# A transformer block with a conditioned conv on one core: order of the first loads, and where the modulation and the first weight parts are made

## What is computed

```python
x = x + conv(x, cond[:, None, :])                  # 32 taps, 256 channels, each by itself, padded left by 31
ada = (cond @ ada_w + ada_b)[:, None, :]           # 6 parts of 256
shift1, scale1, gate1, shift2, scale2, gate2 = jnp.split(ada, 6, axis=-1)
x1 = ln(x) * (1.0 + scale1) + shift1
q, k, v = split(x1 @ qkv_w + qkv_b)                # 256 -> 3 * 2048
a = softmax(q @ k.T * scale) @ v                   # in each sequence of 32 tokens
z = x + gate1 * (a @ out_w + out_b)
x2 = ln(z) * (1.0 + scale2) + shift2
z = z + gate2 * (gelu(x2 @ ffn_w1 + ffn_b1) @ ffn_w2 + ffn_b2)
return x + z
```

## Time and profile before

| | us |
|---|---|
| median of 3 runs | 334.86 (332.93 to 335.1) |
| the profiled execution, whole | 335.84 |
| its span, first to last instruction | 334.0 |
| TensorE busy | 304.7 |
| DVE / ACT / GpSimd busy | 147.5 / 155.2 / 77.1 |
| mean granted clock of TensorE | 0.959 of 2.4 GHz |

### The profile page before, as it was taken

How to read it: one execution, slowest core, us unless ns; L and a number is a source line. 1 busy time by engine, 2 the same in 40 slices (tenths; PEclk the granted TensorE clock), 3 DMA queues, 4 the chain that set the end, 5 groups by cost and what they waited for, 6 DMA issues and landing times.

```text
span 334.0 us, 7536 instructions
## 1 busy us (share of the span) xinstructions
PE 304.7 (91%) x3279; PEld 257.7 (77%) x3279; DVE 147.5 (44%) x235; ACT 155.2 (46%) x259; POOL 77.1 (23%) x68
## 2 busy tenths in 40 slices
PE   0644989999999979999999999999999999899994
PEld 0644879888888868888888888888888687588884
DVE  0612383375344306225332532531625699783232
ACT  3333314555267243536625525644453547742910
POOL 4200185310063020015303005401102345420400
PEclk9955789999999997999999999999999999999999
DMA  6780042010023001003201101210200000000011
GB/s 203 196 312 4 4 126 65 4 65 0 2 72 118 0 4 63 2 0 108 82 0 27 36 0 63 84 45 0 65 2 1 2 2 0 0 2 0 0 65 63
DMA packets 10056, 15.74 MB, mean 47 GB/s; under 512 B 837, under 2 KB 6061, under 8 KB 9901
## 3 DMA queue, kind: packets, MB, share of 16 engines
q1 hardware_dynamic: 9712, 15.24, 14.4%
q10 hardware_dynamic: 317, 0.10, 0.1%
HBM read 14.26 MB, written 1.11 MB: 46 GB/s over the span
## 4 chain that ended last, share of the span: by engine, by line
PE 82%; DVE 9%; DMA 4%; issue 4%; ACT 0%; SPq 0%; POOL 0%; ACTq 0%
PE bank L975 17%; PE bank L976 17%; PE bank L977 17%; PE bank L1051 8%; PE bank L984 5%; PE bank L986 4%; PE bank L985 4%; PE bank L1037 3%; DMA cond_padded<-zrows 2%; PE bank L881 2%; PE bank L911 2%; DMA pool<-cond_padded 2%; PE bank L897 1%; DVE yacc L774 1%; DVE pt L677 1%
## 5 line engine op out<-in xcount | busy, mean ns | idle before, releaser
L302 POOL TENSOR_TENSOR wl<-raw,wh 128x512 fp32r<-128x512 f32 x40 | 52.3, 1330 | 167.5 <-ACT wh L361 167.5
L975 PE MATMUL bank<-x1h,wl 128*128 128x512 f32 (+1 forms) x176 | 67.5, 383 | 1.5 <-DVE x1l L630 1.5
L976 PE MATMUL bank<-x1l,wh 128*128 128x512 f32 (+1 forms) x176 | 65.8, 374 | 0.0
L977 PE MATMUL bank<-x1h,wh 128*128 128x512 f32 (+1 forms) x176 | 65.8, 374 | 0.0
L434 ACT ACTIVATE pool<-bank,bg 128x512 f32<-128x512 f32 x56 | 38.6, 689 | 58.4 <-PE bank L977 58.1
L688 DVE SCALAR_TENSOR_TENSOR ol<-bank,bT,oh 128x512 fp32r<-128x512 f32 x32 | 24.0, 750 | 51.2 <-ACT oh L463 50.2
L975 PEld LDWEIGHTS bank<-x1h,wl 128*128 128x128 f32 x176 | 33.8, 192 | 7.6 <-DVE x1l L630 1.6
L976 PEld LDWEIGHTS bank<-x1l,wh 128*128 128x128 f32 x176 | 34.0, 193 | 5.6 <-issue 0.2
L977 PEld LDWEIGHTS bank<-x1h,wh 128*128 128x128 f32 x176 | 33.9, 192 | 5.7
L1051 PEld LDWEIGHTS bank<-pt,pool 128*128 128x128 f32 x256 | 31.9, 191 | 3.4 <-DVE pt L677 0.8
L1051 PE MATMUL bank<-pt,pool 128*128 128x128 f32 x256 | 32.8, 276 | 0.6 <-DVE ol L688 0.4
(11 more groups left out here) (108 smaller groups left out, 419.2 us busy)
## 6 DMA issues: line engine op xcount, KB each, us to landing
raw<-in_L_cond_qkv_w_dram SPq DMA_DIRECT2D x12, 512.0 KB, 3.9
raw<-in_L_cond_out_w_dram SPq DMA_DIRECT2D x4, 512.0 KB, 3.5
raw<-in_L_cond_ffn_w_dram SPq DMA_DIRECT2D x4, 512.0 KB, 3.5
pool<-in_x_dram SPq DMA_DIRECT2D x2, 512.0 KB, 4.2
pool<-cond_padded SPq DMA_DIRECT2D x4, 256.0 KB, 4.5
adaw<-in_L_cond_ada_w_dram SPq DMA_DIRECT2D x1, 1024.0 KB, 7.6
out_dram<-pool SPq DMA_DIRECT2D x4, 256.0 KB, 2.2
adaw<-in_L_cond_ada_w_dram SPq DMA_DIRECT2D x1, 512.0 KB, 6.3
```

The source lines that it names most:

```text
L302: g.tensor_tensor(wl[:, cols], raw[:, cols], wh[:, cols].bitcast(F32), ALU.subtract)\
L975: pe.matmul(dst, wl[:, w_cols], a_hi, start=start, stop=False)
L976: pe.matmul(dst, wh[:, w_cols], a_lo, start=False, stop=False)
L977: return pe.matmul(dst, wh[:, w_cols], a_hi, start=False, stop=stop)
```

## The change

- SP issues the two writes of `cond_padded` first, then x, then the Toeplitz input, and only then the first third of `adaw` and the biases. ACT's queue keeps the load of `crow`.
- SP waits for two blocks of the conv (`conv_blocks` at 2) before `load_group(0)`; the rest of `adaw` comes after it.
- The modulation has four parts: scale1, shift1, the middle third, the last third. The first two are made by TensorE after the conv, the last two inside `project_chunk(0, ...)`.
- The biases are transposed after conv block 1, into `S_BANK`; `turn(3)` stands behind the projections of q and half of k of chunk 0, `mean(0)` ahead of `turn(1)`.
- GpSimd makes the low parts of q and k ahead of `rstd(0)`. Those of v are made by DVE, and counted on a semaphore of their own (`s_vlow`); GpSimd adds them to `s_wlo`.

TensorE in the front, before: the biases and the modulation stand ahead of the conv (L881), mean(0) (L911) behind 64 of L897's (two turns; here and below each row of a plain f32 matmul is two passes).

The diff, cut to its core:

```diff
-        ADA_PARTS = [(0, ADA1), (ADA1, 2 * ADA1), (2 * ADA1, ADA)]
-        ADA_BANKS = [YB[1], OB[1], YB[1]]
-        ADA_STEPS = [1, 3, 4]
+        ADA_PARTS = [(CT, 2 * CT), (0, CT), (ADA1, 2 * ADA1), (2 * ADA1, ADA)]
+        ADA_BANKS = [OB[0], OB[1], YB[1], OB[1]]
+        ADA_STEPS = [1, 3, 4, 5]
...
+            sp.dma_start(pad_rows(0, T), cond.rearrange("k (g s) -> k g s", g=QB)).then_inc(s_pad, 16)
+            sp.wait_ge(s_zr, 1)
+            sp.dma_start(pad_rows(T, 2 * T - 1), zrows[:, :].rearrange("k (g s) -> k g s", g=QB)).then_inc(s_pad, 16)
             for n in range(HALVES):
                 sp.dma_start(xtok[:, 4 * n:4 * n + 4, :], x_v[:, 4 * n:4 * n + 4, :]).then_inc(s_x[n], 16)
-            load_adaw(0, 0, ADA1 * P)
-            for at, src in ((B_QKV, qkv_b), (B_ADA, ada_b), (B_OUT, out_b), (B_F1, ffn_b1), (B_F2, ffn_b2)):
...
             sp.wait_ge(s_pad, 32)
             for g in range(QB):
                 sp.dma_start(toep_in[T * g:T * (g + 1), :, :].rearrange("p u s -> p (u s)"),
...
+            load_adaw(0, 0, ADA1 * P)
+            for at, src in ((B_QKV, qkv_b), (B_ADA, ada_b), (B_OUT, out_b), (B_F1, ffn_b1), (B_F2, ffn_b2)):
...
+            sp.wait_ge(s_cv, 2)
+            load_group(0)
             load_adaw(1, ADA1 * P, ADA * P)
-            load_group(0)
...
# GpSimd
+            g.wait_ge(s_xq[2], len(SPREADS_POOL))
+            low_parts(0, range(0, 4))
             rstd(0)
-            low_parts(0, range(0, 4))
+            g.wait_ge(s_vlow, 2)
+            g.wait_ge(s_wlo, 4)
+            g.sem_inc(s_wlo, 2)
             rstd(1)
-            low_parts(0, range(4, 6))
...
# ACT
-            a.wait_ge(s_bt, 1)
-            a.activation(bT[:, :], CB[2][:, 0:NBIAS], ACT.Copy).then_inc(s_btc, 1)
...
             conv_copy(0)
+            a.wait_ge(s_bt, 1)
+            a.activation(bT[:, :], S_BANK[:, 0:NBIAS], ACT.Copy).then_inc(s_btc, 1)
+            high_parts(0, range(0, 2))
             conv_copy(2)
-            high_parts(0, range(0, 4))
+            high_parts(0, range(2, 6))
+            group_biases(0, 0, 3)
             xc_copy(0)
-            group_biases(0, 0, 3)
             squares(0)
-            xc_copy(2)
-            high_parts(0, range(4, 6))
             squares(1)
             x1_high(0)
+            xc_copy(2)
...
# DVE
+            for p in (4, 5):
+                cols = slice(PIECE * p, PIECE * (p + 1))
+                v.wait_ge(s_whi, p + 1)
+                v.tensor_tensor(wl[:, cols], raw[:, cols], wh[:, cols].bitcast(F32), ALU.subtract).then_inc(s_vlow, 1)
+            centre(0)
             xc_copy(1)
-            centre(0)
+            modulation(1)
             scale_up(0)
...
             x1_low(1)
+            xc_copy(3)
             modulation(2)
-            one_plus(2, SCALE2)
+            modulation(3)
+            one_plus(3, SCALE2)
             centre(2)
...
# TensorE
+            conv(0)
+            conv(1)
+            pe.wait_ge(s_row[1], 16 * 5)
+            pe.wait_ge(s_co[0], 1)
+            pe.transpose(S_BANK[:, 0:NBIAS], rows[:, :], ident[0:NBIAS, 0:NBIAS]).then_inc(s_bt, 1)
+            conv(2)
+            conv(3)
+            pe.wait_ge(s_adaw[0], 16)
+            pe.wait_ge(s_co[1], 1)
+            modulation(0)
             turn(0)
+            mean(0)
             turn(1)
-            mean(0)
-            turn(2)
+            modulation(1)
             var(0)
             mean(1)
             spread(0)
-            pe.wait_ge(s_adaw[1], 16)
-            modulation(1)
-            turn(3)
+            turn(2)
             var(1)
...
             project_chunk(0, (0, 1))
             spread(1)
+            pe.wait_ge(s_xc[0], 2)
             project_chunk(0, (2,))
-            pe.wait_ge(s_co[1], 2)
+            turn(3)
+            pe.wait_ge(s_adaw[1], 16)
             modulation(2)
             project_chunk(0, (3,))
             pe.wait_ge(s_adat, ADA_STEPS[1])
+            modulation(3)
+            pe.wait_ge(s_adat, ADA_STEPS[3])
             mean(2)
```

More of the change, by code:

```diff
@@ L252, in _ @@
                     .then_inc(s_toep, 16)
+            load_adaw(0, 0, ADA1 * P)
+            for at, src in ((B_QKV, qkv_b), (B_ADA, ada_b), (B_OUT, out_b), (B_F1, ffn_b1), (B_F2, ffn_b2)):
+                n = src.shape[0] // P
+                sp.dma_start(rows[at:at + n, :], src.rearrange("(n p) -> n p", p=P)).then_inc(s_row[1], 16)
+            sp.wait_ge(s_cv, 2)
+            load_group(0)
             load_adaw(1, ADA1 * P, ADA * P)
-            load_group(0)
             with sp.Fori(1, NG) as hg:
@@ L723, in _ @@
                 v.tensor_copy(toep[:, blk, :].rearrange("p s u -> p u s"), toep_in[:, :, blk]).then_inc(s_tp[k], 1)
+            conv_copy(1)
+            conv_copy(3)
             v.wait_ge(s_btc, 1)
@@ L866, in _ @@
                               start=(i == 0), stop=False, is_transpose=True, skip_group_check=True)
-            pe.wait_ge(s_row[1], 16 * 5)
-            pe.transpose(CB[2][:, 0:NBIAS], rows[:, :], ident[0:NBIAS, 0:NBIAS]).then_inc(s_bt, 1)
             def conv(k):
-                if k == 2:
-                    pe.wait_ge(s_btc, 1)
                 if k == 3:
-                    pe.wait_ge(s_adat, 1)
+                    pe.wait_ge(s_cond, 1)
                 pe.wait_ge(s_tp[k], 1)
@@ L957, in _ @@
             pe.wait_ge(s_xq[2], len(SPREADS_POOL))
-            for k in range(NX):
-                conv(k)
+            conv(0)
[8 more added lines that the diff above has]
+            modulation(0)
             turn(0)
+            mean(0)
             turn(1)
-            mean(0)
-            turn(2)
+            modulation(1)
             var(0)
```

13 lines of the change are left out of this document (1 added, 12 removed).

## The result

| | before | after |
|---|---|---|
| median (of runs) | 334.98 us (4) | 337.26 us (4) |
| lowest to highest | 332.93 to 336.39 | 336.28 to 340.0 |
| ratio after/before, 95% | | 1.0112 [1.0058, 1.0166] |
| profiled execution, its span | 335.84, 334.0 us | 336.28, 334.5 us |

The forecast was 330.0 us, 1.5% less, in a range of 327.0 to 334.0; the change costs up to 1% instead. The two profiled executions differ by only 0.44 us.

What follows compares the result with a forecast made beforehand. TensorE's matmuls bound the kernel from 48 us, a chain of waits the 47 us ahead. Terms -3.4 - 0.2 - 3.0 - 1.6 + 3.3 = -4.9 us on 335.84 gave 330.9, as a median 330.0, range 327.0 to 334.0.

Steps and rivals of the forecast that it cites:

- step 1: Start of the conv: earlier pads and Toeplitz load bring the first conv matmul from 17.00 to 13.6, -3.4 us.
- step 2: Length of the conv: 14.7 us against 14.9, -0.2 us; the loaded code fetch moves from first to third round.
- step 3: Conv's end to first projection: 12.5 us instead of 15.5, -3.0 us, from low parts, mean(0), turn(1) and modulation.
- steps 4 and 5: First projection to mean(2): no clock fall, -1.6 us; turn(3) and a modulation moved behind the first projection, +3.3 us.
- rival C: Start of the conv: GpSimd's and the vector engine's copies of x obstruct each other, +3.7 us, 333.7; chance 0.07.
- rival E: Conv's third code fetch waits for the whole held weight load: 332.8 us; chance 0.07.
- (a): First norm: GpSimd's low parts run earlier, so the vector engine's shift and low part are no longer slowed, -3.0 us.
- (b): After the conv: mean(0) waits only for ACT's copy of the first turned part, not turn(1), -1.1 us.
- (c): Between mean(0) and var(0): turn(1) and modulation(1) take 2.1 to 2.7 us where 1.3 went by, +1.1 us.
- Rival F: TensorE stays at the lower clock from first projection through mean(2): +6.9 us, 336.9, slower than before; chance 0.04.
- step 5: Behind the first projection: turn(3), one modulation of 16 passes and a wait at mean(2) now cost time, +3.3 us.

Runs made afterwards that it cites:

- e2: Changed kernel with the pad-row writes put behind crow on ACT's queue and x first on SP's: 1.0001 of the kernel before.
- e1: Changed kernel with GpSimd's copies of x given to ACT (six in all) and the vector engine (ten): 1.0059 of the kernel before.
- e11: Kernel before with the two pad-row writes first on SP's queue and only crow's load on ACT's: 0.9997 of the kernel before.
- e9: Kernel before with e5's edit, e2's queues, Toeplitz ahead of modulation loads, first modulation between conv blocks 2 and 3: 0.9982 of the kernel before.
- e6: Changed kernel with pad rows behind crow on ACT's queue, weights not held, and turn(1) ahead of mean(0): 0.9973 of the kernel before.
- e8: Changed kernel run again with no edit: 1.0045 of the kernel before, median 335.87 us.
- e12: Changed kernel with modulation(2) and turn(3) put back ahead of the first projection: median 339.83 us beside 332.63 of the kernel before; no ratio given.
- e7: Changed kernel with only turn(1) put ahead of mean(0) again: 1.0065 of the kernel before.
- e3: Changed kernel without SP's wait for two conv blocks, so weights aren't held: 1.0034 of the kernel before.
- e4: Changed kernel with weights held until all four conv blocks are done, high and low parts moved later: 1.0048 of the kernel before.
- e5: Kernel before with only GpSimd's four low parts of q and k moved ahead of rstd(0): 0.9917 of the kernel before, median 331.76 us.
- e10: Changed kernel with modulation(0) and (1) between the third and fourth conv blocks: 1.0157 of the kernel before, four executions.

## Why the prediction was wrong

The forecast of 330.0 us missed the measured 337.26. In the profiled executions mean(2) came 6.7 us later than forecast (58.80 against 52.1): 4.4 us by step 1, 0.2 by step 2, 1.8 by step 3 and 0.2 by steps 4 and 5.

**Step 1 failed, by 4.4 us, the largest miss.** Its failing sentence is that the copies of x "no longer matter: the Toeplitz load is last". The pads were written by 5.15, inside the forecast's 4 to 6, and Toeplitz landed at 14.0 against 13.0. But x landed at 9.3, not 7.3. I put that to Toeplitz, issued at 5.15 and moving beside it: in e2, where it goes at 8.31, x is there at 6.6, though x itself is issued 1.2 us earlier there as well. And the copies took 7.96 instead of 4.96 us. That was rival C, which I gave 0.07 with a start of 17.3; measured 18.04. That its number comes so near is luck: it had x 1.9 us too early and the two sets of copies one after the other, 9.3 us, where they took 7.96. I argued against it from the pace of one copy alone, 0.62 us for 512 elements, when I had no row with both engines copying; e1 showed that this was no evidence. The Trainium skill (SBUF — State Buffer, Who interferes with whom) has the lock with GpSimd for copies only in a mode with two ports. Whether these copies are in that mode no run here shows; the rows of after, e2 and e11 (7.9 us each) against e1 (6.14 for ten) show a slowing of the vector engine's, whatever its mechanism, and GpSimd's took 1.3 us each in the first three, 1.04 in before.

No run brought step 1's 3.4 us. The earliest start was 15.56 (e9), 1.4 us before that of before. e1 and e9 start the conv 1.6 and 1.4 us earlier than after and before, and end it no earlier, or lose it to work placed there. e2 and e6 start it at 16.0 and 16.1 and end it at 31.3 and 31.4, before at 31.9. e2's ratio is 1.0001 against 1.0045 of e8, on another chip and with intervals that overlap: some half a per cent, if anything. So the collision explains why the conv started late; that it alone turned the sign isn't shown.

**Step 2 had the mechanism and under-sized a term.** The stops stand after 204, 127 and 127 pairs, the long one moved to the third round, as forecast. The third round took 6.1 us in e12, 6.36 in after and e2, 7.45 in e8 and e1 and 7.7 in e7, where one row had given 5.9: rival E's direction (0.07), a fetch that waits for the held load. e3 and e4 show that the load is the cause. In after's profile the two rounds ahead were 0.4 us quicker than forecast, so the length came out only 0.2 us over; in e8's the third round was another 1.1 us longer.

**Step 3 was right in (a), wrong in its price of modulation(0) and in (b), and (c) was at the upper end.** The shift and low part are at 0.75 and 0.76, 3.0 us as forecast. But modulation(0) didn't hide beside the conv's last copy, where I had it at 0.95 us and "costs nothing": it took 1.92 at the low pace, of which some 0.6 show (from the conv's end to turn(0) 1.77 us against 1.17). mean(0) took 2.08, priced by its 1.37 in before. (c), turn(1) and modulation(1), had 2.1 to 2.7 us, the low pace of the turn included; from the end of mean(0) to var(0) 2.6 went by. So modulation(0) and mean(0), priced by rows of a faster TensorE, make some 1.3 of the 1.8 us. The 16 passes of modulation(0) and (1) had stood at 13.47 in before, where TensorE waited for Toeplitz, and took 1.91 us there. Cut out of that hole they take 1.92 + 1.08, of which some 0.6 + 1.1 are on the chain.

**Steps 4 and 5 were right**: the pace doesn't fall again (0.12 us for each matmul), the moved work costs its 3.4 us, 11.54 against a forecast of 11.3. Rival F (slower through a low clock from the first projection on, 0.04) ended on the right side for the wrong reason: the low pace lay ahead of the projection, not behind it. The price of step 5, which I had right, weighs more than it looked. After reaches mean(2) 4.1 us behind e5 (58.80 against 54.66), which has only part (a) and leaves that work where it was: 0.5 at the conv's end, 0.2 from there to the first projection, 3.5 behind it. And with the start, the hold and the turns repaired, e6 is still 0.8 us behind e5 there.

**Open.** How long the low pace lasts behind the conv isn't explained: until 37.4 in before, 36.3 in e6, 41 in after, 54 in e12. Nor is it why some executions of the changed kernel reach 339 to 344 us when before never passed 337.33. No such execution of after was profiled, but two of its variants were: e2's, of 340.87 us, still has its projections 0.21 us apart at 54.5 and 0.12 apart only from 55.7 on; e7's, of 341.56, until 57.4. In after the same matmuls are 0.12 apart from 47.5 on, right behind the first. So a longer low pace goes with the long executions; what starts or ends it isn't known. Nor did any run add to e5, one at a time, the two moves that are left, the first modulation behind the conv and the middle one with turn(3) behind the first projection: how the cost divides between them is read from landmarks, not shown by the time.

## What to carry to other kernels

Before work is moved out of a place, look at what the engine did there: sixteen passes in a hole cost nothing, and eight of the same passes on the chain behind a stretch of small matmuls took double (1.92 us against half of 1.91). A transfer that comes earlier starts other work earlier as well, so ask which copies on which engines will now overlap, and measure such a pair before the sum rests on it. And try each part of a change alone: here one moved line (e5) held all of the gain, 0.8%, and the rest of the change, taken together, cost it and more.

## What the hardware showed that I had not expected

- Copies of 32x512 f32 by the vector engine and GpSimd at once: 0.96 us (median) and up to 1.36 instead of 0.59, and 1.33 instead of 1.04. Over eight copies that is 3.0 us, as much as GpSimd's two-input operations cost the shift and the low part of the first norm, though less for each operation.
- The recorded clock can say 1.00 while TensorE runs at its slow pace: 64 passes of turn in 1.94 us at a recorded 1.00, 1.10 us for the same at 44.77 in the same trace.
- In straight code of 32x32 matmuls TensorE stops after each 128 pairs of weight load and matmul, which I read as the fetch of the next block of code. Beside the load of 3 MB a round took 4.8 us (e3, the first) to 7.7 (e7, the third), without it 3.3 to 3.9. With matmuls put in between there were further stops (e10).
- The stop at the loop's entry, 2.06 us, is there in some executions and not in others (e8), and the pace behind it varies as well.
